# Query and key parts kept for 1024 rows in two slots, stored by half of the heads

## What is computed

```python
Q = (x @ WQ + bQ).reshape(b, s, h, dh).transpose(0, 2, 1, 3)
K = (x @ WK + bK).reshape(b, s, h, dh).transpose(0, 2, 1, 3)
V = (x @ WV + bV).reshape(b, s, h, dh).transpose(0, 2, 1, 3)
scores = jnp.einsum('bhqd,bhkd->bhqk', Q, K) / scale
...
A = jax.nn.softmax(scores, axis=-1)
Z = jnp.einsum('bhqk,bhkd->bhqd', A, V)
out = jnp.einsum('bhsd,de->bse', Z, WO) + jnp.float32(h) * bO
...
x = x + _L0_attn_ref(_L0_cond_ref(x, fside_Bx2_0, condB_angle), ...)
x = x + _L0_ffn_ref(_L0_cond2_ref(x, ...), ...)
```

## Time and profile before

| | us |
|---|---|
| median of 3 runs | 1002.67 |
| lowest, highest | 998.75, 1004.54 |
| the profiled execution, whole | 1009.86 |
| its span on the core, which the views show | 1008.0 |
| PE busy | 746.9 |
| DVE busy | 525.3 |
| ACT busy | 359.8 |
| POOL busy | 286.6 |

### The profile page before, as it was taken

One profiled execution on the slowest core, in us unless ns is written; L12 is line 12 of the kernel. 1 busy time (PEld: TensorE's weight loads), 2 busy tenths in 40 slices (PEclk: granted clock), 3 DMA queues, 4 the chain that ended last, 5 costly groups with the idle time before them and its releaser, 6 DMA issues.

```text
span 1008.0 us, 13583 instructions
## 1 busy us (share of the span) xinstructions
PE 746.9 (74%) x4027; PEld 442.9 (44%) x4027; DVE 525.3 (52%) x1069; ACT 359.8 (36%) x912; POOL 286.6 (28%) x268
## 2 busy tenths in 40 slices
PE   0350222636868888889999897899679999999992
PEld 0340111232323333534446343577436777666772
DVE  6163555669677766576787761544513333333320
ACT  0122333361546644455474573212112222232220
POOL 0113454643865613200200024111531111122111
PEclk9965555676878889999999997999879999999996
DMA  8598888797943003999801015776479999999953
GB/s 265 190 300 298 275 301 286 251 267 247 262 151 132 33 2 126 276 291 320 300 1 44 2 40 205 255 223 193 142 237 338 303 292 303 291 294 301 290 157 94
DMA packets 136205, 216.12 MB, mean 214 GB/s; under 512 B 10357, under 2 KB 102058, under 8 KB 135978
## 3 DMA queue, kind: packets, MB, share of 16 engines
q1 hardware_dynamic: 114808, 150.78, 46.3%
q0 software_dynamic: 16784, 61.51, 19.4%
q10 hardware_dynamic: 4546, 3.08, 1.0%
HBM read 160.87 MB, written 56.37 MB: 216 GB/s over the span
## 4 chain that ended last, share of the span: by engine, by line
PE 44%; DVE 6%; DMA 4%; issue 3%; POOL 3%; SPq 1%; ACT 1%; POOLq 0%; DVEq 0%; ACTq 0%
PE psum L1482 12%; PE psum L1466 12%; PE psum L1407 4%; PE psum L1237 3%; PE psum L1473 3%; DVE arena L1708 3%; PE psum L1421 2%; POOL pairs_x L1001 2%; DMA arena<-pairs_x 2%; PE psum L1370 2%; PE psum L1250 1%; DMA arena<-qk_rows 1%; PE psum L1457 1%; PE psum L1359 1%; PE psum L1259 1%
## 5 line engine op out<-in xcount | busy, mean ns | idle before, releaser
L1160 ACT ACTIVATE arena<-psum 128x512 f32<-128x512 f32 (+3 forms) x384 | 170.6, 492 | 137.2 <-PE psum L1426 102.9
L1708 DVE TENSOR_REDUCE arena<-psum 128x2 f32<-128x1024 f32 (+2 forms) x192 | 176.1, 953 | 58.0 <-PE psum L1243 44.8
L1209 ACT ACTIVATE arena<-psum,b_cols 128x128 f32<-128x128 f32 x312 | 84.7, 383 | 271.6 <-PE psum L1473 267.2
L1466 PE MATMUL psum<-arena 128*128 128x512 f32 x312 | 148.0, 619 | 9.5 <-issue 9.5
L1482 PE MATMUL psum<-arena 128*128 128x256 f32 x624 | 146.3, 389 | 6.0 <-ACT arena L1209 6.0
L1009 POOL DMA_INDIRECT results<-arena,home x39 | 61.4, 1574 | 265.8 <-DVE arena L2033 240.5
L1237 PE MATMUL psum<-arena 96*128 96x512 bf16 (+3 forms) x384 | 110.6, 354 | 34.9 <-DVE arena L1708 17.3
L1482 PEld LDWEIGHTS psum<-arena 128*128 128x128 f32 x624 | 119.2, 196 | 23.0 <-issue 7.3
L1421 PE MATMUL psum<-arena 99*128 99x512 bf16 (+3 forms) x384 | 115.9, 340 | 10.8 <-ACT arena L1160 5.2
L2014 DVE COPY arena<-psum 128x1024 f32<-128x1024 f32 x39 | 47.7, 1224 | 109.1 <-PE psum L1466 109.1
L1466 PEld LDWEIGHTS psum<-arena 128*128 128x128 f32 x312 | 59.1, 200 | 71.3 <-issue 71.3
(11 more groups left out here) (208 smaller groups left out, 975.1 us busy)
## 6 DMA issues: line engine op xcount, KB each, us to landing
arena<-L_ffn_W SPq DMA_DIRECT2D x78, 1024.0 KB, 5.6
pairs_x<-zeros SPq DMA_DIRECT2D x4, 4160.0 KB, 25.8
arena<-qk_rows SPq DMA_DIRECT2D x16, 768.0 KB, 11.3
table<-arena SPq DMA_DIRECT2D x20, 384.0 KB, 10.0
qk_rows<-arena SPq DMA_DIRECT2D x16, 384.0 KB, 5.4
arena<-pairs_x SPq DMA_DIRECT2D x39, 130.0 KB, 4.6
qk_rows<-arena SPq DMA_DIRECT2D x16, 256.0 KB, 5.7
padded<-arena SPq DMA_DIRECT2D x2, 1328.0 KB
```

Source lines behind the costliest of these rows:

```text
L1160: nc.scalar.activation(probs[at % 2][h][:, q0:512], banks[turn % SCORE_BANKS][:, q0:512], ACT.Exp, scale=DH ** -0.5).then_inc(exp_done, 1)
L1209: ins = nc.scalar.activation(hidden_t[:, f], banks[3 + f // 4][:, (f % 4) * P:(f % 4 + 1) * P], ACT.Relu, bias=b1_cols[:, bass.ds(e, 1), f])
L1466: ins = t_.matmul(banks[half], x_t[:, c], w1_slot[u][:, c, half * 512:(half + 1) * 512], start=c == 0, stop=c == DC - 1)
L1708: return v.reduce_max(part[:, 2 * pair:2 * pair + 2, qb], psum[:, first:first + 2, 0:keys], AX_X)
```

## The change

The three parts are kept for the whole 1024 rows of a kind, in two slots: `parts[0]` for queries, `parts[1]` for keys. The space is the same. Both chunks of a kind write into their half of the slot. One store now covers both chunks, so that each row is 2 KB and there are six stores a c and batch in place of twelve. A store of a kind waits for both its chunks. ACT's first part of a chunk with c = 1 waits until the kind's stores of c = 0 have landed. For batch 0, SP now loads stacks 0 and 1 together once c = 0 is stored, waits until stack 0 has landed, and only then stores c = 1. In batch 1 the order on SP is as before.

```diff
-PART_SLOTS = 4
+PART_SLOTS = 2
-        parts = [tile([3, 512], BF16) for u in range(PART_SLOTS)]
+        parts = [tile([3, S], BF16) for u in range(PART_SLOTS)]
+        def part_of(j, t):
+            kind, c, half = chunk_place(j)
+            return parts[kind][:, t, half * 512:(half + 1) * 512]
...
-            def store_parts(b, chunks):
-                for j in chunks:
-                    kind, c, half = chunk_place(j)
-                    sp.wait_ge(parts_ready, b * QK_CHUNKS + j + 1)
-                    u = j % PART_SLOTS
-                    heads = P // DH
+            def store_parts(b, c):
+                heads = P // DH
+                for kind in range(2):
+                    sp.wait_ge(parts_ready, b * QK_CHUNKS + (2 * c + kind) * 2 + 2)
                     rows = qk_rows[kind, b * H + c * heads:b * H + (c + 1) * heads].rearrange("h d i s -> (h d) i s")
                     for i, t, n_parts, copies in PART_RUNS[kind]:
                         n = n_parts * copies
-                        part = parts[u][:, t:t + n_parts]
-                        sp.dma_start(rows[:, i:i + n, half * 512:(half + 1) * 512],
-                                     part if copies == 1 else part.broadcast_to([P, n, 512])
-                                     ).then_inc(parts_stored[u], 16)
+                        part = parts[kind][:, t:t + n_parts]
+                        sp.dma_start(rows[:, i:i + n], part if copies == 1 else part.broadcast_to([P, n, S])
+                                     ).then_inc(parts_stored[kind], 16)
...
-                    store_parts(b, range(PART_SLOTS))
+                    store_parts(b, 0)
                     for u in range(2):
                         sp.wait_ge(strip_stored[u], 48 * (JB + 1))
                     parts_are_stored(b, 0)
-                    load_stack(0, 0)
-                    store_parts(b, range(PART_SLOTS, QK_CHUNKS))
-                    load_stack(1, 1)
+                    for g in range(2):
+                        load_stack(g, g)
+                    sp.wait_ge(stack_in[0], STACK_IN)
+                    store_parts(b, 1)
...
-            store_parts(1, range(PART_SLOTS))
+            store_parts(1, 0)
...
-            store_parts(1, range(PART_SLOTS, QK_CHUNKS))
+            store_parts(1, 1)
...
-                        if n >= PART_SLOTS:
-                            act.wait_ge(parts_stored[j % PART_SLOTS], PART_STORES * (n // PART_SLOTS))
-                        nc.scalar.activation(parts[j % PART_SLOTS][:, 0], banks[j], ACT.Identity,
+                        if c:
+                            act.wait_ge(parts_stored[kind], PART_STORES * c)
+                        nc.scalar.activation(part_of(j, 0), banks[j], ACT.Identity,
...
-                act.wait_ge(parts_stored[j % PART_SLOTS], PART_STORES * (2 + j // PART_SLOTS))
+                act.wait_ge(parts_stored[kind], PART_STORES * (2 + c))
```

More of the change, by code:

```diff
@@ L982, in _ @@
                 pool.wait_ge(max_read, USE_OF["project", j, 1] + 1 + 2)
-                g_.tensor_copy(parts[j % PART_SLOTS][:, 1], resid[j % 2]).then_inc(halved, 1)
+                g_.tensor_copy(part_of(j, 1), resid[j % 2]).then_inc(halved, 1)
                 pool.wait_ge(halved, QK_CHUNKS + j + 1)
-                g_.tensor_tensor(parts[j % PART_SLOTS][:, 2], resid[j % 2], parts[j % PART_SLOTS][:, 1],
+                g_.tensor_tensor(part_of(j, 2), resid[j % 2], part_of(j, 1),
                                  ALU.subtract).then_inc(parts_ready, 1)
@@ L1146, in first_part @@
                 act.wait_ge(max_scored, USE_OF["project", j, 1] + 1)
-                act.wait_ge(parts_stored[j % PART_SLOTS], PART_STORES * (2 + j // PART_SLOTS))
-                nc.scalar.activation(parts[j % PART_SLOTS][:, 0], banks[side_banks(USE_OF["project", j, 1])],
+                act.wait_ge(parts_stored[kind], PART_STORES * (2 + c))
+                nc.scalar.activation(part_of(j, 0), banks[side_banks(USE_OF["project", j, 1])],
                                      ACT.Identity, bias=bqk[:, kind, c:c + 1]).then_inc(first_parts, 1)
@@ L1691, in what_it_leaves @@
                 v.scalar_tensor_tensor(out=resid[j % 2], in0=banks[j], scalar=bqk[:, kind, c:c + 1],
-                                       in1=parts[j % PART_SLOTS][:, 0], op0=ALU.add,
+                                       in1=part_of(j, 0), op0=ALU.add,
                                        op1=ALU.subtract).then_inc(proj_read, 1)
@@ L1696, in second_part @@
                 dve.wait_ge(proj_read, b * QK_CHUNKS + j + 1)
-                v.tensor_copy(parts[j % PART_SLOTS][:, 1], resid[j % 2]).then_inc(halved, 1)
+                v.tensor_copy(part_of(j, 1), resid[j % 2]).then_inc(halved, 1)
             def third_part(b, j):
                 dve.wait_ge(halved, b * QK_CHUNKS + j + 1)
-                v.tensor_tensor(parts[j % PART_SLOTS][:, 2], resid[j % 2], parts[j % PART_SLOTS][:, 1],
+                v.tensor_tensor(part_of(j, 2), resid[j % 2], part_of(j, 1),
                                 ALU.subtract).then_inc(parts_ready, 1)
@@ L1808, in side @@
                     v.scalar_tensor_tensor(out=resid[i % 2], in0=bank, scalar=bqk[:, kind, c:c + 1],
-                                           in1=parts[i % PART_SLOTS][:, 0], op0=ALU.add,
+                                           in1=part_of(i, 0), op0=ALU.add,
                                            op1=ALU.subtract).then_inc(max_read, 1)
```

2 lines of the change are left out of this document (1 added, 1 removed).

## The result

The changed kernel took 1015.3 us (median of 4 runs, 1011.98 to 1017.81), the kernel before 1002.5 us in the same session (998.75 to 1004.54). The ratio is 1.0137 with a 95% interval of 1.0105 to 1.0169, so 12.8 us slower. The prediction was 1006.2 us with a range to 1010.7. The time lies outside it, beyond even the +5 to +8 us of rival 1.

What follows compares the result with a forecast made beforehand. PE was taken to bound the kernel, waiting on the chain of chunk 3's parts, their stores and the stack load. +1.5 + 0.3 + 1.7 = +3.5 us on the 1002.67 median gave 1006.2 us, range 1000.2 to 1010.7.

Steps and rivals of the forecast that it cites:

- rival 1: Batch 0: gathers hold back the keys' stores, landing near 218 instead of 215.2; +5 to +8 us in all; chance 0.20.
- The queries were to land at 205.1: Batch 0: queries' stores issued at 199.57 land 1.5 + 4.0 us later, delaying DVE's chunk 4 step by 0.3 us.
- 84 ns for 2 KB: Store price per 2 KB packet, from a line through 1 KB and 6 KB packets; 4.0 us a kind.
- The order on SP: Batch 0: stack 1 arrives some 5 us earlier, but nobody uses it before 253.63, so nothing gained.
- PE was to wait 2.7 us: Batch 1: with the stack loads landing 1.7 us later, PE waits 2.7 in place of 1.00 us.
- the added 1.7 us: Batch 1: PE's longer wait for the later stack load, priced one for one; bounds +1.4 and +4.5.
- 5.5 + 2.9 - 0.5 = 7.9 us: Batch 0, keys' stores: time alone, plus loss to gathers, less unused queue capacity; issued 207.25, landing 215.2, +1.7.
- The 2.9 us that chunk 3 lost to the gathers: Batch 0: chunk 3's stores took 6.6 us where 3.7 is the time alone; the same loss assumed for the keys.
- Rows 10: Batch 0 profile rows: gathers took 96.5% of engines from 212 to 216; read as order of issue, against alternation.
- 1.9 us for the small stores: Batch 0: upper bound for one gather ahead of the small stores of the negated maxima; forecast took +0.3.
- The cover by ACT and DVE: Batch 0: DVE ends 224.5, PE's first pair due 227.3; 3 us of slack, gone if keys land after 218.
- the forecast had +1.8: Batch 0 terms: +1.5 for the later stack 0 load and +0.3 for gather packets flowing over the small stores.

Runs made afterwards that it cites:

- e2: Kernel before, but in batch 0 both stacks are loaded ahead of the stores of c = 1, which wait for stack 0; ratio 0.9999.
- base: Kernel before, run again unchanged as a null; ratio 0.9984.
- x4: Changed kernel's two slots, but stores chunk by chunk in 1 KB rows and the old order on SP; ratio 1.0036 to the kernel before.
- the test of the hold: Changed kernel with POOL's gather(2) held until stack 0 is in; ratio 1.0068 to the kernel before.
- after: The changed kernel itself, in three series; ratios 1.0137, 1.0101 and 1.0130 to the kernel before.
- e1: Changed kernel with the old order on SP in batch 0 (stack 0, stores of c = 1, stack 1); ratio 1.0091 to the kernel before.
- x7: Changed kernel with the row-maximum pairs for n = 4 begun one step later in n = 3; ratio 1.0045 to the kernel before.
- x11: Changed kernel with 4 bytes between the parts in a slot, so the keys' stores go in 2 KB packets; ratio 1.0112 to the kernel before.
- x1: Changed kernel, but in batch 1 the stores of c = 0 go out chunk by chunk again; ratio 1.0034 to the kernel before.
- x2: Kernel before with its narrow stores, but in batch 1 each store waits for both chunks of its pair; ratio 1.0053.
- x8: Kernel before with the row-maximum pairs for n = 4 begun one step later in n = 3; ratio 1.0032.
- x3: Changed kernel, but in batch 0 the stores of c = 0 go out chunk by chunk again; ratio 1.0059 to the kernel before.
- x6n: Kernel before with POOL's gather(2) held until stack 0 is in; ratio 0.9953, in a second series 0.9956.
- x12: Two slots, chunk-by-chunk stores, old order on SP, and gather(2) held until stack 0 is in; ratio 0.9963 to the kernel before.

## Why the prediction was wrong

**Right by its steps.** The queries were to land at 205.1; ACT went on at 204.84, though 6.0 us after their issue at 198.86 in place of 5.5 us after 199.57, so part of this is luck. SP issued 24 stores (three shapes, eight times each), and 84 ns for 2 KB holds: 1.033 of 32 us by 391 packets is 84.5 ns, for the queries. The keys' stores didn't go out in 2 KB packets as forecast. gather(3) was to start near 244 and started at 244.23, without a longer wait at L1425. The order on SP was priced at nothing, and e2 gave 0.9999. In batch 1 the loads were to start 1.7 us later relative to the stores' issue: 398.04 to 403.33 is 5.3 us, before 399.31 to 403.15 was 3.8, so 1.5; PE was to wait 2.7 us and waited 2.6.

**Batch 1, the term that was too small.** The wait of 2.7 us was right and its price wrong. The sum took the added 1.7 us as the whole cost, and the clock stood in no term. The wait takes the clock down at its place for 3.4 to 6.8 us, in all eight executions; in six of them a second fall follows. Over these eight, batch 1 lasted 53.6 to 57.3 us, 56.1 on the mean. The undisturbed ones (before, base, e2, x4) took 51.2: +4.9. All twelve others, in five of which the later fall comes too, took 50.8 to 53.7, 52.0 on the mean: +4.1. Either is far from +1.7.

**Batch 0, the stores.** The failing step is 5.5 + 2.9 - 0.5 = 7.9 us for the keys' stores; it was 10.4. The 2.9 us that chunk 3 lost to the gathers was carried over as it stood, though the kind has twice the bytes and goes on longer beside them. Rows 10 were read as order of issue; but the 96.5% there only says that nothing but gathers was left by 212 to 216, since chunk 3 was nearly through. Rival 1 named the mechanism and its landing, 218 against 217.3, and the test of the hold confirms it (10.4 to 6.2 us). Its price of +5 to +8 was short too: it had 1.9 us for the small stores, which came to nothing, and took batch 1 at the same 1.7.

**Batch 0, the load and the cover.** With the stores late, the load meets no gathers and takes 9.3 us, as rival 1 had it (8.9), so PE starts at 226.69. This gives back 2.9 of the 3.8 us. The cover by ACT and DVE is gone at this landing, as forecast for keys later than 218: DVE ends L1723 at 226.76, PE's first product is at 226.69. It cost nothing yet, since DVE's first maximum at 227.31 still waited 0.55 us for PE. The mean of batch 0 over the seven wide kernels without split or hold (after three times, e1, x7, x11 and, split in batch 1 only, x1) is 65.5 us, of the four narrow ones in the old order (before, base, x2, x8) 62.5 (61.2 to 63.8, against 64.9 to 66.4): +3.0 where the forecast had +1.8.

**The sum.** 3.0 + 4.1 = 7.1 us, or 7.9 against the undisturbed executions, of 10.1 to 13.7 measured in the three series (ratios 1.0101, 1.0137, 1.0130). Behind the mark of n = 4 the eight executions with the long wait took 559.1 us on the mean to the end and the twelve others 557.4, some 1.7 us more; in e1, x3 and x11 a fall of the clock reaches over this mark, and they took 561.0 to 561.5. **Some 1 to 5 us stay open.** The splits gained more in the medians (x1 some 8 us, x3 some 5) than their own traces show in the two stretches (3 and 1), but such a gain has its interval of several us. Part may lie where one profiled execution can't show it: between the small stores of n = 1 and those of n = 3 the five executions of the two kernels took 98.0 to 105.2 us, with 9 to 26 us at the lower clock. Whether the changed kernel falls there more often wasn't tried.

## What to carry to other kernels

A wait of TensorE that grows from 1 to 3 us in a dense stretch is to be priced with the clock behind it; here the 1.7 us of longer wait came to 4 to 5 us. A store that something waits for should be kept apart from a queue of long gather packets: the two queues share the engines, and holding back a gather that nobody needs yet was worth more here (4.4 to 4.7 us on the kernel before) than any form of the store. Joining two transfers into one makes both wait for the later part, which is free only where nothing waits for their landing.

## What the runs showed of the hardware

- Stores whose rows lie side by side in SBUF and in HBM went out as merged packets of up to 6 KB: 124 packets with 0.69 MB in the changed kernel, and 1536 packets more where a gap of 4 bytes parts the rows (x11). Making all packets 2 KB gained nothing (1.0112).
- Every wait of PE of 2.3 to 3.7 us for the stack of n = 4 took its clock to the lower level (8 executions), no wait of up to 1.1 us for it did (12). But further on, in 11 of all 20 executions, a fall came within 3 us of two waits for VectorE of 1.0 and 0.8 us close together (0.9 and 1.0 us in x7), with no longer one in between. What sets the 11 apart from the 9 is not shown.
- The issue of an indirect gather on POOL took 0.94 to 1.51 us. What makes it longer is not shown: in x4 it took 0.98 and 0.95 us while DVE was busy (203.47, 204.76), before it took 1.51 with DVE busy (206.28).
- Where a gather's packets moved first, chunk 3's stores of 1 KB rows needed 10.6 us from the first issue to the landing (x4), with the gathers held 4.1 (x6n) and 4.0 (x12).
